# Head statistics of a graph layer, computed through TensorE and PSUM instead of on VectorE

## The chip, the cores and the metric

The kernel runs on one core of one Trainium2 chip. The metric is the device time of one launch in microseconds (us), the median of three runs. The core has five engines with queues of their own: TensorE (PE in the profile, its weight loads PEld), VectorE (DVE), ScalarE (ACT), GpSimd (POOL) and SyncE (SP), which only issues DMAs. They meet through semaphores.

## The reference, cut to what matters

The input x has 3125 rows (nodes) of 256 numbers; 53125 edges (src, dst, sorted by dst) carry three numbers each.

```
xn  = layernorm(x)
gnn = xn + segment_sum(messages(xn[src], edge_attr), dst)      # the edge loop
mix : heads of 32 columns (H = 8, hc = 32), q = xn
      k = (q - mean) / (std(ddof=1) + 1e-5) * kw + kb          # per row and head
      v = (q - mean) / (std(ddof=1) + 1e-5) * vw + vb
      out = q @ (k.T @ v / N) + xn
x = x + gnn + mix
x = x + expert_ffn(layernorm(x))                               # top 2 of 8 experts
```

For k and v each row of xn has to be centred and divided by its standard deviation within each of its 8 heads. This is what the text calls the head statistics. The sums over all rows of the products of these normalised rows (two 128x128 blocks) and their column sums are all that the rest needs.

## The kernel before, in words

**Rows.** The 3125 rows lie as 125 partitions by J = 25 tiles of 256 columns. NB = 5 batches of JB = 5 tiles are loaded; ScalarE normalises batches 0 to 2 (L1017), VectorE batches 3 and 4 (L1330), and SyncE writes them to DRAM as `xn_rows` (L455). VectorE then works out the edges' unit vectors (L1336 to L1342), with one square root on ScalarE between (L1034).

**Head stage (about 38 to 79 us of the trace).** Per batch of five tiles: VectorE sums each head (L1365), forms the deviations `dev` (L1366); ScalarE squares them (L1064); VectorE sums the squares (L1372); ScalarE takes the root (L1070); VectorE adds EPS, takes the reciprocal (L1377, L1378) and multiplies into `hx` in two parts (L1383); TensorE adds hx.T @ [hx, 1] for each tile and half into two banks of `ps3` (L699), two 128-column matmuls a tile. Each fp32 matmul is two records in the trace, a transpose is one. `hx` holds one batch, so L1383 waits until TensorE has used the batch before it. Ahead of this TensorE and ScalarE compose the weights of the edge loop from small 64x64 matrices, in turns: TensorE L664 to L685, ScalarE L1042 to L1059 (`lin_t`, `tp_t`, `ba_t`, ..., `w_sc`).

**Edge loop (about 79.6 to 625 us).** G = 104 groups of 512 edges, software pipelined in `step(i, k)`, which each of TensorE, ScalarE and VectorE has in its own order. GpSimd gathers the source rows, four indirect DMAs of 128 rows a group (L556), into a ring of RING = 10 groups `xg`. It needs all of `xn_rows` written, the group's indices in `idx_st` (written by ScalarE in `stage_idx`, L1030, five groups at a time) and the ring's slot free (`turn_sums`, which TensorE raises once a step). Indices of groups 0 to 9 are staged ahead of the loop, those of groups 10 to 14 in step 4, behind everything that ScalarE does in that step:

```
if k + AHEAD >= RING and (k + AHEAD) % HALF == 0:      # AHEAD = 6, HALF = 5
    stage_idx(i, k + AHEAD)
```

VectorE starts a group with its products (L1431, `prod`), two steps ahead of the step's number; nothing of the loop precedes the end of the head stage in the queues of TensorE, ScalarE and VectorE. ScalarE also clears the six parts of the accumulator `agg` in the first steps (L1148).

**After the loop** come the second layernorm and the gate, and then 56 expert tiles, in the order of TensorE (L961, L975).

Of the kernel before, what the change touches and what calls it, by code (L numbers as in the profile page):

```python
# [52 lines left out]
def gps_layer_kernel(nc, t, out, dbg=None):  # L53
# [42 lines left out]

    COLS = 5
# [14 lines left out]
    with ExitStack() as ctx:  # L112
# [32 lines left out]
        dev = sb(early, "dev", [P, J, D])  # L145
        compose = ExitStack()
        wsm = sb(compose, "wsm", [M, len(names), M])
        lin_t = sb(compose, "lin_t", [M, 128])
        tp_t = sb(compose, "tp_t", [M, 2, 128])
        ba_t = sb(compose, "ba_t", [M, 128])  # L150
        d_t = sb(compose, "d_t", [M, 128])
        c_t = sb(compose, "c_t", [M, 128])
        w_v = sb(compose, "w_v", [M, M])
        rep = sb(compose, "rep", [M, 2, 128])
        compose.close()
        sq = sb(early, "sq", [P, JB * H, HC])
# [12 lines left out]
        hx = sb(early, "hx", [P, JB, 2, 129])  # L169
# [40 lines left out]

        loop = ExitStack()
# [96 lines left out]

        PARTS = ((0, 3), (3, JB))
        head_ready, head_used = ([sem(f"{n}{k}") for k in (0, 1)] for n in ("head_ready", "head_used"))  # L310
        kv_ready, sel_padded = sem("kv_ready"), sem("sel_padded")

        class GroupSems:

            def __init__(s, tag, ring):
                s.ring = ring
                s.gathered = [sem(f"{tag}gathered{i}") for i in range(ring)]
                (s.idx, s.prod, s.dot, s.zt_ps, s.zt_sb, s.f_ps, s.o0, s.hid, s.hid_ps, s.hid_t, s.scores, s.neg_top,
                 s.exp, s.hot, s.norm, s.coef, s.eo, s.sel, s.scattered, s.added, s.turn_heads, s.turn_sums) = (  # L320
                    sem(tag + n) for n in ("idx", "prod", "dot", "zt_ps", "zt_sb", "f_ps", "o0", "hid", "hid_ps", "hid_t",
                                           "scores", "neg_top", "exp", "hot", "norm", "coef", "eo", "sel", "scattered",
                                           "added", "turn_heads", "turn_sums"))

        main, wide = GroupSems("", RING), GroupSems("wide_", 1)
        loc_ready, agg_final = sem("loc_ready"), sem("agg_final")
# [71 lines left out]
        def mix_t_ps(s):  # L398

            return ps2[:, 1, s * 512 + 260:s * 512 + 260 + 2 * P].rearrange("q (h p) -> q h p", h=2)  # L400

# [241 lines left out]
        def _(pe):  # L643
# [17 lines left out]
            pe.wait_ge(w_loaded, 16 * len(names))  # L661
            pe.wait_ge(consts_ready, 10)
            pw = ps1[:, 0, :]
            pe.transpose(pw[0:M, 0:M], W["lin_src_w1"], ident[0:M, 0:M])  # L664
            pe.transpose(pw[0:M, M:128], W["lin_src_w0"], ident[0:M, 0:M]).then_inc(w_mm, 1)
            pe.wait_ge(w_copied, 1)
            for k, (a, b) in enumerate((("tp1_w11", "tp1_w00"), ("tp1_w10", "tp1_w01"))):
                o = 128 + 128 * k
                pe.matmul(pw[0:M, o:o + M], W[a], lin_t[:, 0:M], start=True, stop=True)
                mm = pe.matmul(pw[0:M, o + M:o + 128], W[b], lin_t[:, M:128], start=True, stop=True)  # L670
            mm.then_inc(w_mm, 1)
            pe.wait_ge(w_copied, 2)
            pe.matmul(pw[:, 0:M], tp_t[:, 0, :], W["lin_hidden_w0"], start=True, stop=True)
            pe.matmul(pw[0:M, 128:256], W["lin_hidden_w0"], tp_t[:, 0, :], start=True, stop=True)
            pe.matmul(pw[0:M, 256:384], W["lin_hidden_w1"], tp_t[:, 1, :], start=True, stop=True).then_inc(w_mm, 1)
            pe.wait_ge(w_copied, 3)
            pe.matmul(pw[:, 0:M], ba_t[:, :], W["tp2_w00"], start=True, stop=False)
            pe.matmul(pw[:, 0:M], d_t[:, :], W["tp2_w11"], start=False, stop=True)
            pe.matmul(pw[:, M:128], c_t[:, :], W["tp2_w11"], start=True, stop=True)
            pe.matmul(pw[:, 128:192], ba_t[:, :], W["tp2_w01"], start=True, stop=False)  # L680
            pe.matmul(pw[:, 128:192], c_t[:, :], W["tp2_w10"], start=False, stop=True)
            pe.matmul(pw[0:M, 192:256], d_t[:, 0:M], W["tp2_w10"], start=True, stop=True).then_inc(w_mm, 1)
            pe.wait_ge(w_copied, 4)
            pe.matmul(pw[:, 256:320], rep[:, 0, :], w_v[:, :], start=True, stop=True)
            pe.matmul(pw[:, 320:384], rep[:, 1, :], w_v[:, :], start=True, stop=True).then_inc(w_mm, 1)  # L685

            pe.wait_ge(short_ready, 1)
            pe.wait_ge(base_ready, 2)
            pe.transpose(ps1[0:1, 1, 256:384], short[:, 0:1], ident[:, :]).then_inc(short_col, 1)  # L690
            pe.wait_ge(edge_cols_taken, len(tables))
            pe.wait_ge(banks_cleared, 1)
            for b in range(NB):
                for k, (j0, j1) in enumerate(PARTS):
                    pe.wait_ge(head_ready[k], b + 1)
                    for jj in range(j0, j1):
                        for c in range(2):

# [296 lines left out]
        def _(act):  # L995
# [41 lines left out]
            for k in range(0, RING, HALF):  # L1037
                stage_idx(0, k)
# [855 lines left out]
```

## Time and profile before

| | us |
|---|---|
| median of 3 runs | 1160.52 |
| the three runs | 1160.38, 1160.52, 1164.48 |
| span of the profiled execution | 1163.6 |
| TensorE busy | 1056.7 (91%) |
| VectorE busy | 762.1 (65%) |
| ScalarE busy | 623.8 (54%) |
| GpSimd busy | 634.9 (55%) |

The profile is of one execution, whose span, from its first to its last instruction, is 1163.6 us; no other time is listed for it, and it lies 0.9 us under the highest of the three runs and 3.1 us over the median. Starts in the rows count from the start of the span. A share of busy time is a mean over stages that are bound by different things, so the stages are read apart. The granted TensorE clock is given as a share of 2.4 GHz: 1.00 is 2.4 GHz and 0.50 is 1.2 GHz.

### The profile page before, as it was taken

What the parts mean: (1) busy time and instruction counts of PE and PEld (TensorE: products, weight loads), DVE (VectorE), ACT (ScalarE), POOL (GpSimd) and SP (SyncE); (2) the same over time, 40 slices, a digit from 0 to 9 for tenths busy, and PEclk for the clock granted to TensorE, in tenths of its full rate; (3) what the DMA queues carried; (4) which work ended last, traced back from release to release, by engine and by line L of the source; (5) the groups of instructions that cost most, each with busy time, mean ns of one, the idle gap of its engine ahead of it and who ended that gap; (6) DMA issues with size and microseconds to landing.
All of it is one profiled execution on the core that took longest, in us unless ns stands there. A gap on an engine that the chain in (4) does not pass through costs nothing.

```text
span 1163.6 us, 27165 instructions
## 1 busy us (share of the span) xinstructions
PE 1056.7 (91%) x8001; PEld 1003.1 (86%) x8002; DVE 762.1 (65%) x1942; ACT 623.8 (54%) x1948; POOL 634.9 (55%) x700
## 2 busy tenths in 40 slices
PE   1377999999999999999998977799999999999993
PEld 1267999999999999999997975699999999999992
DVE  6888999999999999999984658333333333333330
ACT  3329555555555555555554760655555555555550
POOL 2474777777777777777731300444444444444431
PEclk9568999999999999999997989899999999999997
DMA  6532333333333333333320334583222222222224
GB/s 160 160 91 68 111 109 112 103 108 103 109 113 105 110 109 109 109 111 105 105 61 5 106 117 181 177 296 65 36 36 34 38 36 36 36 36 36 35 29 124
DMA packets 47378, 108.51 MB, mean 93 GB/s; under 512 B 13814, under 2 KB 24871, under 8 KB 45160
## 3 DMA queue, kind: packets, MB, share of 16 engines
q0 software_dynamic: 30720, 69.24, 24.2%
q1 hardware_dynamic: 16308, 37.47, 9.9%
q10 hardware_dynamic: 308, 1.28, 0.3%
q8 instruction: 21, 0.34, 0.1%
q14 instruction: 21, 0.17, 0.0%
HBM read 90.88 MB, written 20.27 MB: 96 GB/s over the span
## 4 chain that ended last, share of the span: by engine, by line
PE 44%; issue 15%; DVE 12%; POOL 10%; ACT 9%; DVEq 4%; DMA 4%; SPq 0%; POOLq 0%; ACTq 0%
PE ps L961 17%; PE ps L975 16%; POOL xg L556 10%; ACT e L1115 5%; DMA xg<-xn_rows,idx_st 3%; DVEq L1551 2%; PE ps L813 1%; PE ps L864 1%; DVE neg_top L1452 1%; PE ps L860 1%; PE ps L945 1%; ACT agg L1148 1%; PE ps L889 1%; PE ps L699 1%; PE ps L861 1%
## 5 line engine op out<-in xcount | busy, mean ns | idle before, releaser
L556 POOL DMA_INDIRECT xg<-xn_rows,idx_st x416 | 417.5, 1004 | 170.3 <-issue 124.6
L813 PE MATMUL ps<-sel,xg 128*128 128x120 f32 x2496 | 298.5, 276 | 3.8 <-DVE sel L1540 1.3
L813 PEld LDWEIGHTS ps<-sel,xg 128*128 128x128 f32 x2496 | 286.8, 192 | 10.0 <-issue 9.2
L1266 ACT ACTIVATE ht_sb<-ps,b_cur 128x128 f32<-128x128 f32 x448 | 127.9, 369 | 162.5 <-PE ps L961 162.5
L961 PEld LDWEIGHTS ps<-xst,w_st 128*128 128x128 f32 x1792 | 210.1, 193 | 5.6 <-issue 2.8
L961 PE MATMUL ps<-xst,w_st 128*128 128x128 f32 x1792 | 210.6, 276 | 2.3 <-ACT ht_sb L1266 1.7
L1115 ACT ACTIVATE e<-ps,neg_top 128x65 f32<-128x65 f32 x416 | 125.4, 316 | 161.8 <-DVE neg_top L1452 143.7
L975 PE MATMUL ps<-w_sb,ht_sb 128*128 x896 | 202.8, 379 | 0.8 <-DVE y_sb L1845 0.8
L626 POOL DMA_INDIRECT sum_rows<-y_sb,put_st x56 | 108.4, 1935 | 145.6 <-DVE y_sb L1848 135.4
L975 PEld LDWEIGHTS ps<-w_sb,ht_sb 128*128 128x128 f32 x896 | 166.7, 191 | 21.4 <-issue 1.2
L1845 DVE TENSOR_TENSOR y_sb<-ps,b_bc 128x256 f32<-128x256 f32 x56 | 23.8, 425 | 184.2 <-PE ps L975 184.2
L1256 ACT ACTIVATE w_st<-w_sb 128x1024 f32 x56 | 116.1, 2074 | 33.3 <-DVE etile L1813 32.3
L741 PE MATMUL ps<-w_f,zt 128*128 128x128 f32 x832 | 113.1, 280 | 0.0
L1431 DVE TENSOR_TENSOR prod<-xg,edge_r 128x768 f32<-128x768 f32 x104 | 99.3, 955 | 11.5 <-DMA xg<-xn_rows,idx_st 8.1
L741 PEld LDWEIGHTS ps<-w_f,zt 128*128 128x128 f32 x832 | 104.0, 196 | 0.6
L1540 DVE TENSOR_TENSOR sel<-hot,ps 128x800 f32<-128x800 f32 x104 | 102.2, 982 | 0.3
L1439 DVE TENSOR_REDUCE xg<-prod 128x256 f32<-128x768 f32 x104 | 99.0, 952 | 0.2
L1832 DVE TENSOR_SCALAR w_st<-w_sb 128x1024 f32 x56 | 61.6, 1100 | 42.1 <-PE ps L961 39.1
L612 POOL DMA_INDIRECT xs_sb<-expert_in_rows,take_st x56 | 61.0, 1089 | 48.5 <-POOL take_st L608 48.5
L1115 ACT ACTIVATION_READ_ACCUMULATOR e<-ps,neg_top 128x1 f32 x416 | 85.7, 206 | 0.0
L726 PE MATMUL ps<-ident,xg 128*128 128x128 f32 x416 | 66.3, 283 | 11.2 <-DVE xg L1439 8.8
L1087 ACT ACTIVATE zt<-ps 128x512 f32<-128x512 f32 x104 | 63.5, 611 | 12.4 <-PE ps L726 12.4
(271 smaller groups left out, 1363.1 us busy)
## 6 DMA issues: line engine op xcount, KB each, us to landing
w_sb<-in_L_ffn_W SPq DMA_DIRECT2D x16, 1024.0 KB, 6.8
xg<-xn_rows,idx_st POOLq DMA_INDIRECT x416
x_sb<-in_x SPq DMA_DIRECT2D x5, 560.0 KB
xn_rows<-xn_sb SPq DMA_DIRECT2D x5, 560.0 KB
xn_t<-xn_rows SPq DMA_DIRECT2D x25, 112.0 KB
expert_in_rows<-xf_sb SPq DMA_DIRECT2D x12, 224.0 KB
sum_rows<-x_sb SPq DMA_DIRECT2D x12, 224.0 KB
out<-sum_rows SPq DMA_DIRECT2D x3, 560.0 KB
```

What stands on the lines that cost most here:

```text
L556: pool.indirect_dma_start(xg[:, s, tt, M:M + D], None, xn_dram, bass.IndirectOffsetOnAxis(ap=idx_st[:, s, tt:tt + 1], axis=0)).then_inc(ma ...
L626: pool.indirect_dma_start(sum_dram, bass.IndirectOffsetOnAxis(ap=put_st[:, s:s + 1], axis=0), y_sb[:, s, :], None, compute_op=ALU.add).the ...
L741: mm = pe.matmul(f_bank(s)[:, tt * 128:(tt + 1) * 128], zt[:, s, tt * 128:(tt + 1) * 128], w_f[:, :], start=True, stop=True)
L813: mm = pe.matmul(ps3[:, s, col:col + n], xg[:, r, tt, lhs0:lhs0 + 128], sel[:, s, lo:lo + n], start=(tt == 0), stop=(tt == TG - 1))
L961: mm = pe.matmul(h_of(c), w1_st[:, s, kc, c, :], xst[:, s, kc, :], start=(kc == 0), stop=(kc == 1))
L975: mm = pe.matmul(ps1[:, 1, 0:D], ht_sb[:, o % 2, c, :], w2_sb[:, bass.ds(e, 1), c, :].rearrange("p e d -> p (e d)"), start=(c == 0), stop= ...
L1115: ins = act.activation(e0[:, s, tt, :], score_ps(s)[:, tt * (M + 1):(tt + 1) * (M + 1)], ACT.Exp, bias=neg_top[:, s, tt:tt + 1], accum_out ...
L1256: act.activation(w1_st[:, o % 2, 1, :, :], w1_columns(e, 1), ACT.Copy).then_inc(w1_half1, 1)
L1266: ins = act.activation(ht_sb[:, o % 2, c, :], h_of(c), ACT.Gelu, bias=b1_cur[:, o % 2, c:c + 1])
L1431: return dve.tensor_tensor(prod[:, :, :, :], xg[:, s, :, 128:320].rearrange("p t (u m) -> p t u m", m=3), r, ALU.mult)
L1439: dve.tensor_reduce(xg[:, o % RING, :, 0:M], prod[:, :, :, :], AX.X, ALU.add).then_inc(main.dot, 1)
L1540: return dve.tensor_tensor(sel[:, s, 0:TG * 5 * WIN].rearrange("p (t k w) -> p t k w", t=TG, k=5), hot[:, s, :, :].unsqueeze(2).to_broadca ...
```

## The change

The head stage is laid out anew; what it computes stays the same.

- TensorE transposes each half tile of `xn_sb` into PSUM (`turn_pair`, two tiles at a time, 13 pairs); ScalarE copies the transposed pair to SBUF (`copy_turned`); TensorE multiplies it with the 128x128 matrix `centre` = identity minus the mean over each head, so that the deviations come out in PSUM (`centre_pair`). The tiles are taken in the order 15 to 24, then 0 to 14 (`TURNED`).
- ScalarE takes the squares from PSUM into `sq` (four pairs deep) and copies the deviations from PSUM into `hx`, which now holds all 25 tiles.
- VectorE only sums the squares (`mean_squares`, per pair), and per four tiles adds EPS, takes the reciprocal and multiplies `hx` in place (`quotients`). The head sums of `xn` and `dev` (L1365, L1366) are gone, with the tile `dev` and the waits for one batch's `hx`.
- TensorE's head sums come per four tiles (`head_sums`), from the sixth pair on.
- The composing of the weights is put between the pairs: the first part behind the first two turns, then behind pairs 0, 1 and 3 on TensorE, and the copies behind pairs 0, 1 and 3 on ScalarE. ScalarE stages the indices of the first ten groups behind pair 2 (`stage_first`), where it did so ahead of everything.
- VectorE's small preparations (L1348 to L1355) and the making of `centre` go ahead of the wait for the square root of the edge lengths; the flags and `w_f`, `w_hi`, `w_lo` go between the quotients.
- The small composing tiles now lie over the loop's tiles instead of the head stage's. A few semaphores that the main loop did not use are gone.

```diff
+            turn_lin()
+            pe.wait_ge(edge_cols_taken, len(tables))
+            turn_pair(0)
+            turn_pair(1)
+            compose_first()
+            pe.wait_ge(centre_ready, 1)
+            COMPOSED_AFTER = {0: compose_hidden, 1: compose_second, 3: compose_upper, 4: turn_short}
+            for q in range(NQ):
+                centre_pair(q)
+                turn_pair(q + 2)
+                if q in COMPOSED_AFTER:
+                    COMPOSED_AFTER[q]()
+                if q >= 5 and q % 2 == 1:
+                    if q == 5:
+                        pe.wait_ge(banks_cleared, 1)
+                    head_sums((q - 5) // 2)
+            for f in range((NQ - 5) // 2, NF):
+                head_sums(f)
...
-            act.wait_ge(edges_ready, 1)
-            for k in range(0, RING, HALF):
-                stage_idx(0, k)
...
+            def copy_turned(q):
+                act.wait_ge(rows_turned, q + 1)
+                n = len(PAIRS[q])
+                act.activation(xtt[:, q % 2, 0:n, :, :].rearrange("f t h p -> f (t h) p"),
+                               turned_ps(q)[:, 0:n, :, :].rearrange("f t h p -> f (t h) p"), ACT.Copy).then_inc(turned_copied, 1)
+            def squares(q):
+                act.wait_ge(rows_centred, q + 1)
+                if q >= SQUARES:
+                    act.wait_ge(head_var, q - SQUARES + 1)
+                act.activation(sq[:, q % SQUARES, 0:n, :], centred_ps(q)[:, 0:n, :], ACT.Square).then_inc(head_sq, 1)
+            def deviations_out(q):
+                act.activation(hx[:, 2 * q:2 * q + n, :, 0:128].rearrange("p t c f -> p (t c) f"),
+                               centred_ps(q)[:, 0:n, :].rearrange("p t (c f) -> p (t c) f", f=128), ACT.Copy).then_inc(head_dev, 1)
...
+            copy_lin()
+            copy_turned(0)
+            COPIED_AFTER = {0: copy_first, 1: copy_hidden, 2: stage_first, 3: copy_second}
+            for q in range(NQ):
+                copy_turned(q + 1)
+                squares(q)
+                deviations_out(q)
+                if q in COPIED_AFTER:
+                    COPIED_AFTER[q]()
+                if q >= 3 and q % 2 == 1:
+                    head_deviation((q - 3) // 2)
+            for f in range((NQ - 2) // 2, NF):
+                head_deviation(f)
...
+            dve.scalar_tensor_tensor(out=centre[:, :], in0=head_block[:, :], scalar=-float(N) / HC, in1=ident[:, :],
+                                     op0=ALU.mult, op1=ALU.add).then_inc(centre_ready, 1)
...
-            def heads(b):
-                own(dve.tensor_reduce(total, xh, AX.X, ALU.add))
-                dve.scalar_tensor_tensor(out=dev[...], in0=total..., scalar=-1.0 / HC, in1=xh,
-                                         op0=ALU.mult, op1=ALU.add).then_inc(head_dev, 1)
...
+            def mean_squares(q):
+                dve.wait_ge(head_sq, q + 1)
+                dve.tensor_reduce(hstat[:, 1, 2 * q * H:(2 * q + n) * H],
+                                  sq[:, q % SQUARES, 0:n, :].rearrange("p t (h c) -> p (t h) c", c=HC), AX.X, ALU.add).then_inc(head_var, 1)
+            def quotients(f):
+                dve.wait_ge(head_std, f + 1)
+                own(dve.tensor_scalar(hstat[:, 0, hb], hstat[:, 2, hb], EPS, None, ALU.add))
+                own(dve.reciprocal(hstat[:, 1, hb], hstat[:, 0, hb]))
+                dve.wait_ge(head_dev, FOURS[f][-1] + 1)
+                dve.tensor_tensor(rows, rows, hstat[:, 1, hb]..., ALU.mult).then_inc(head_ready, 1)
...
+            for f in range(NF + 1):
+                if f < NF:
+                    for q in FOURS[f]:
+                        mean_squares(q)
+                if f >= 1:
+                    quotients(f - 1)
+                if f == 3:
+                    upper_weights()
+                if f == 4:
+                    flags()
```

## Rows read from the trace of the kernel before

**Rows 1.** The page, its first line.
```profile
span 1163.6 us, 27165 instructions
```

**Rows 2.** The chain that ended last (start us, us, what), its longest pieces.
```profile
68.27 6.85 PE ps L699 x32
...
302.98 2.73 DMA xg<-xn_rows,idx_st
...
595.44 4.33 DMA xg<-xn_rows,idx_st
```

**Rows 3.** Line L556, the gathers: what ended GpSimd's idle time (us, times).
```profile
L556 POOL DMA_INDIRECT xg<-xn_rows,idx_st x416: 942/946/2270, 41.4 to 595.4; - x139
  issue: 124.6, 409
```

**Rows 4.** Timeline of GpSimd (start us, us, engine, line, [idle before]): gathers 1, 12, 40, 41.
```profile
41.38 2.27 POOL L556 DMA_INDIRECT xg<-xn_rows,idx_st  x1 [32.87 <-DMA xn_rows<-xn_sb]
57.70 1.97 POOL L556 DMA_INDIRECT xg<-xn_rows,idx_st  x1 [0.30 <-issue]
97.40 0.95 POOL L556 DMA_INDIRECT xg<-xn_rows,idx_st  x1 [0.30 <-issue]
109.68 1.37 POOL L556 DMA_INDIRECT xg<-xn_rows,idx_st  x1 [11.33 <-ACT idx_st L1030]
```

**Rows 5.** Timeline of VectorE: a product of group 100.
```profile
583.20 0.96 DVE L1431 TENSOR_TENSOR prod<-xg,edge_r 128x768 f32<-128x768 f32 x1 [0.21 <-DMA xg<-xn_rows,idx_st]
```

**Rows 6.** Groups by form, 20 to 82 us: busy us, mean ns | idle before.
```profile
L1366 DVE SCALAR_TENSOR_TENSOR dev<-hstat,xn_sb 125x1280 f32<-125x1280 f32 x5 | 7.5, 1492 | 0.2
L1372 DVE TENSOR_REDUCE hstat<-sq 125x40 f32<-125x1280 f32 x5 | 7.4, 1481 | 2.5 <-ACT sq L1064 2.5
L1365 DVE TENSOR_REDUCE hstat<-xn_sb 125x40 f32<-125x1280 f32 x5 | 7.3, 1469 | 0.0
L1383 DVE TENSOR_TENSOR hx<-dev,hstat 125x768 f32<-125x768 f32 x5 | 4.8, 960 | 1.7 <-PE ps L699 1.6
L1383 DVE TENSOR_TENSOR hx<-dev,hstat 125x512 f32<-125x512 f32 x5 | 3.4, 688 | 0.7 <-PE ps L699 0.7
L1378 DVE RECIPROCAL hstat<-hstat 125x40 f32<-125x40 f32 x5 | 2.0, 404 | 0.2
```

**Rows 7.** Timeline of ScalarE ahead of the head stage.
```profile
25.15 7.48 ACT L1017 ACTIVATE xn_sb<-x_sb,ln_tmp,rstd 125x256 f32<-125x256 f32 x15 [0.68 <-DVE ln_tmp L1326]
32.54 0.53 ACT L1034 ACTIVATE edge_len<-edge_len 128x416 f32<-128x416 f32 x1
38.35 0.33 ACT L1030 ACTIVATE idx_st<-edge_src 128x20 int32<-128x20 int32 x2 [5.28 <-DVE edge_r L1342]
```

**Rows 8.** Timeline of TensorE and VectorE: head sums, the loop's first product.
```profile
61.82 4.67 PE L699 MATMUL ps<-hx 125*128 125x129 f32 x20 [1.72 <-DVE hx L1383]
76.23 2.50 PE L699 MATMUL ps<-hx 125*128 125x129 f32 x20 [0.23 <-DVE hx L1383]
79.64 0.90 DVE L1431 TENSOR_TENSOR prod<-xg,edge_r 128x768 f32<-128x768 f32 x1
```

**Rows 9.** Groups by form of ScalarE, 110 to 600 us: a 512-column copy from PSUM.
```profile
L1087 ACT ACTIVATE zt<-ps 128x512 f32<-128x512 f32 x97 | 59.2, 611 | 0.0
```

**Rows 10.** Stretches: length, busy PE, PEld, DVE, ACT, POOL, then granted clock, DMA, GB/s.
```profile
38.80:48.00 9.20, 6.91 (x31) 5.62 (x31) 6.57 (x8) 3.23 (x13) 5.41 (x5) 0.50 0.42 106
60.00:67.00 7.00, 4.78 (x21) 4.37 (x20) 6.86 (x10) 1.68 (x4) 5.78 (x5) 0.50 0.29 85
75.00:79.00 4.00, 3.50 (x29) 3.12 (x28) 2.98 (x10) 0.00 (x0) 3.09 (x4) 1.00 0.33 98
88.00:95.00 7.00, 3.59 (x30) 3.19 (x30) 6.22 (x12) 7.00 (x10) 5.48 (x6) 0.99 0.33 94
```

**Rows 11.** Timeline of TensorE, 84.3 to 88.3 us: transposes, then matmuls.
```profile
86.83 1.09 PE L726 MATMUL ps<-ident,xg 128*128 128x128 f32 x4 [0.32 <-ACT zt L1087]
87.71 0.85 PE L741 MATMUL ps<-w_f,zt 128*128 128x128 f32 x4
```

More of the change, by code:

```diff
@@ L95, in gps_layer_kernel @@
     MIX = {0: 0, 3: 1, 6: 2}
+    TURNED = list(range(ACT_NB * JB, J)) + list(range(ACT_NB * JB))
+    PAIRS = [range(q, min(q + 2, J)) for q in range(0, J, 2)]
+    NQ = len(PAIRS)
+    FOURS = [range(q, min(q + 2, NQ)) for q in range(0, NQ, 2)]
+    NF = len(FOURS)
+    SQUARES = 4
     COLS = 5
@@ L144, in gps_layer_kernel @@
         xn_sb = sb(early, "xn_sb", [P, J, D])
[L145 to L156, printed above, removed]
+        hx = sb(early, "hx", [P, J, 2, 129])
         kv_tmp = sb(early, "kv_tmp", [128, 2, 2, 128])
@@ L671, in _ @@
[L671 to L690, printed above, removed]
-            pe.wait_ge(edge_cols_taken, len(tables))
[L692 to L697, printed above, removed]
-                            mm = pe.matmul(ps3[:, c, 0:129], hx[:, jj, c, 0:128], hx[:, jj, c, :], start=False, stop=False,
-                                           skip_group_check=True)
-                    mm.then_inc(head_used[k], 1)
+            def turn_lin():
+                pe.wait_ge(w_loaded, 16 * len(names))
+                pe.wait_ge(consts_ready, 10)
+                pe.transpose(pw[0:M, 0:M], W["lin_src_w1"], ident[0:M, 0:M])
+                pe.transpose(pw[0:M, M:128], W["lin_src_w0"], ident[0:M, 0:M]).then_inc(w_mm, 1)
@@ new lines, in compose_upper, with turn_short, turn_pair @@
+            def compose_upper():
+                pe.wait_ge(w_copied, 4)
+                pe.matmul(pw[:, 256:320], rep[:, 0, :], w_v[:, :], start=True, stop=True)
+                pe.matmul(pw[:, 320:384], rep[:, 1, :], w_v[:, :], start=True, stop=True).then_inc(w_mm, 1)
+            def turn_short():
+                pe.wait_ge(short_ready, 1)
+                pe.wait_ge(base_ready, 2)
+                pe.transpose(ps1[0:1, 1, 256:384], short[:, 0:1], ident[:, :]).then_inc(short_col, 1)
+            def turn_pair(q):
+                if q >= NQ:
+                    return
+                tiles = [TURNED[k] for k in PAIRS[q]]
+                if max(tiles) >= ACT_NB * JB:
+                    pe.wait_ge(xn_ready, max(tiles) // JB - ACT_NB + 1)
+                else:
+                    pe.wait_ge(xn_ready_act, max(tiles) // JB + 1)
+                if q >= 2:
+                    pe.wait_ge(turned_copied, q - 1)
+                for t, j in enumerate(tiles):
+                    for h in range(2):
+                        mm = pe.transpose(turned_ps(q)[:, t, h, :], xn_sb[:, j, h * 128:(h + 1) * 128], ident[0:P, 0:P])
+                mm.then_inc(rows_turned, 1)
@@ L1067, in deviation, with copy_lin @@
-            def deviation(b):
-                act.wait_ge(head_var, b + 1)
-                hb = slice(b * JB * H, (b + 1) * JB * H)
-                act.activation(hstat[:, 2, hb], hstat[:, 1, hb], ACT.Sqrt, scale=1.0 / (HC - 1)).then_inc(head_std, 1)
-            act.wait_ge(w_copied, 4)
-            for b in range(NB):
-                squares(b)
-                deviation(b)
+            def copy_lin():
+                act.wait_ge(w_mm, 1)
+                act.activation(lin_t[:, :], pw[0:M, 0:128], ACT.Copy).then_inc(w_copied, 1)
```

223 lines of the change are left out of this document (128 added, 95 removed).

## The prediction, made before the changed kernel was run

> **What bounds the kernel now.** I read the head of the page first: a span of 1163.6 us [rows 1], 3.1 us over the median of the runs; the sum below is made against the span and then carried to the median. The change ends where the edge loop begins, so the questions are when the loop begins and what the loop hands on of an earlier start.
>
> The chain of waits gives the first half of the answer. Around 68 to 79 us it lies on the head sums of TensorE, from about 303 us to the loop's end it comes back again and again to the landing of gathers [rows 2]. The gathers are issued by GpSimd at a pace of their own: 0.95 us each, and 0.30 us of issue between two, 124.6 us of issue over 409 of them [rows 3], so that four take 5.0 us at least. By the mean of 1004 ns on the page a group of four takes 5.2 us. The loop's later products wait for exactly these [rows 5]. So the loop's end is the end of the gather stream, and that stream has one hole: the gathers of groups 0 to 9 end at 98.35 us (97.40 + 0.95), and group 10 starts at 109.68, 11.33 us later, when ScalarE has staged the next indices in step 4 [rows 4]. Step 4 hangs on the loop's start at 79.64 us [rows 8], 30.0 us before it. From this: an earlier loop by X us moves the 41st gather and with it the whole rest by X, as long as the first 40 gathers are done by then. The first 40 took 57.0 us from 41.38 us [rows 4].
>
> The head stage itself is VectorE's and TensorE's. VectorE spends 7.3 + 7.5 + 7.4 us on three passes, 4.8 + 3.4 on the products and 2.0 on reciprocals [rows 6]: 32.4 of the 39 us from its first head sum to the last head sum on TensorE at 78.73 (76.23 + 2.50) [rows 8]. TensorE's granted clock there is 0.50, that is 1.2 GHz, and only at the end 1.00 [rows 10].
>
> **What is removed.** Two of VectorE's three passes go, 14.8 us, and the waits for one batch's hx, 2.3 us [rows 6]. What VectorE still does (7.4 of squares, some 8 of products, 3 of reciprocals and additions) is 18.5 us, and no longer the bound.
>
> **What is added, TensorE.** I count in records, as the profile does: an fp32 matmul is two, a transpose one. Per tile: 2 transposes, 2 centring matmuls (4), 2 head sums (4), so 10. For 25 tiles 250. Composing and the flag's transpose are 32, as 31 stand in the stretch of composing [rows 10]. Eight transposes (the first two pairs) run at about 27 us, when the tiles of VectorE's batch are normalised and everybody else is busy: free. That leaves 274 records from 33 us on. A record costs 0.107 us at 2.4 GHz (the 20 from 76.23 us took 2.50, less the tail of the last) and 0.213 us at 1.2 GHz (the 20 from 61.82 us took 4.67) [rows 8, 10]. So TensorE alone needs 29.3 us at the full clock and 58.4 us at the half clock. This is the term that decides.
>
> **What is added, ScalarE.** Three passes of 500 or 512 columns a pair from PSUM, by the row of such a copy 0.61 us [rows 9], of which about 0.08 overlap with the next, so 0.53: 1.6 us a pair, against 2.14 us of TensorE at the full clock (20 records) and 4.3 at the half. The shapes with squares, and with gaps of one element in `hx`, are not in the trace; below they can hardly be under 0.53, since the copy passes the same columns; above, L1017 takes 0.49 us for 256 columns (7.48 us for 15) [rows 7], which would be 0.98 a pass and 2.9 us a pair. I take 0.53, from the row nearest in source and size.
>
> **The schedule at the start.** ScalarE is free at 33.1 us (32.54 + 0.53) [rows 7], VectorE's preparations fit into its wait for that root. From there TensorE and ScalarE take turns, since composing is threaded between pairs. In us: copy of `lin_t` to 33.3; first composing matmuls, 5 records at half clock, to 34.5; centring of pair 0, 8 records, 36.2, landed 36.5; squares and copy 37.6; `tp_t` 37.9; composing 8 records 39.8; centring of pair 1 41.5, landed 41.7; squares and copy 42.9; `ba_t` and its neighbours 43.5; composing 13 records, now at the full clock, 45.0; centring of pair 2 45.8; squares and copy 47.2; **indices staged 47.5**; pair 3's three passes 49.2; last copies of weights 50.1; last composing 50.8. Here I chose that the clock rises at about 42 us, since TensorE is then nearly without a gap from 38 us on. If it rises by 37 us, the two marks are 45.8 and 49.1.
>
> **The rest of the head stage.** After 50.8 us there remain 17 tiles of centring (68 records), 13 of transposes (26), all head sums (100), one for the flag: 195 records, 20.9 us at the full clock, and ScalarE with 9 x 1.6 + 0.6 lies under it. At the end the last pairs run dry: reduction 0.6, root 0.2, addition and reciprocal 0.5, product 1.2 us of VectorE in front of the last head sums, of which some 2.1 us are not covered. So 50.8 + 20.9 + 2.1 = 73.8 us, against 78.73 before. **X = 4.9 us** (early clock: 72.2 and X = 6.5).
>
> **The gathers.** Before, indices were there at 38.7 us and the gathers began with the landing of `xn_rows` at 41.38. Now the indices are at the 9th place of ScalarE's queue, and GpSimd, behind them, starts at 47.5: 6.1 us later. The first 40 gathers then end near 47.5 + 57.0 = 104.5. Against this, some of them are drawn out by VectorE: the one at 57.70 us took 1.97 instead of 0.95 [rows 4], beside a pass of L1366. Five such passes go; I take 2 us off (bounds 0 and, all of what the 40 took over 1.25 us each, 7): 102.5. Step 4 comes at 109.7 - 4.9 = 104.8. So the 2.3 us between are what is left of the hole, and the late indices cost nothing yet. They cap what an earlier loop can bring at 109.7 - 102.8 = 6.9 us with the late clock, 8.5 with the early one.
>
> The Trainium skill, GPSIMD Engine Reference (its table of the engine), says that GpSimd shares its SBUF interfaces with VectorE and contends with instructions of two SBUF inputs; the row at 57.70 us agrees. Without the rule the 2 us would be 0, and the sum stays.
>
> **Sum.** The 41st gather moves by -4.9 us, the loop's end with it, and nothing behind the loop changes: span 1163.6 - 4.9 = 1158.7, and at the median 1160.5 - 4.9 = **1155.6 us**. A measurement here tells about 0.5% (5.8 us) from no change, so the likeliest outcome lies just inside "no change".
>
> **Rivals.**
>
> 1. *The clock rises early and stays, the hole closes.* X = 6.5 to 8, capped by the gathers: 1152.5 to 1154.5. For it: TensorE has 3.6 us without a gap from 33.5 us. Against it: in the composing stretch before it had 6.9 us of work in 9.2 and stayed at 0.50 [rows 10]. Chance 0.38.
> 2. *ScalarE becomes the bound.* At 0.98 a pass 9.5 pairs cost 28 us after 50.8 or later: 79 to 80 us, no gain, about 1160 to 1162. For it only L1017, which has a bias and a scale per row and reads SBUF. The same time comes out if the clock falls back twice between pairs, 1.7 to 2.5 us each. Chance 0.10.
> 3. *TensorE stays at 1.2 GHz (the slower side).* Then 33.5 + 58.4 and some 4 us of turns: the head stage ends at 96 us instead of 78.7, step 4 moves by +17, and the time is 1177.7. For it: through all of the old head stage, with 4.8 us of work in 7, the clock was 0.50 [rows 10]. Against it: in the new order TensorE at 1.2 GHz is short of time and never idle after 50 us, and the one stretch without gaps before, 6.85 us of head sums from 68.27 us, ended at 2.4 GHz [rows 2, 10]. It decides from the point where the clock is still low after 55 us; each 5 us of delay beyond costs 2.5 us, and 10 us of it already take the gain. Chance 0.12.
>
> A transpose might not count as work: 4 of 20 records of a steady pair. In the trace the clock was back at 0.99 from 88 us [rows 10], right after a stretch with four transposes among matmuls [rows 11], so here they do not keep it down. The Trainium skill, TensorE: Matmul & The Clock Gate (Part 4: PE-mode transpose), says that the full clock does not engage for transposes. By that rule rival 3 would be the outcome; the trace speaks against it, which is why its chance is 0.12 and not more.
>
> **How the numbers follow.** The forecast as worked out, a gain of 2.5 to 5.8 us, has 0.40; rival 1 has 0.38, all of it over 0.5% faster; rival 2 has 0.10, no change; rival 3 0.12, slower. So faster 0.38, no change 0.50, slower 0.12. The range: down to the cap, 1160.5 - 8.5 = 1152; up over rival 2 and the scatter of the runs, 1163. Rival 3 is left outside.
>
> **What would show it.** The granted clock between 33 and 60 us (rises by 37 or 42: right; later: rival 3). ScalarE's 38 passes near 0.6 us each. The first gather at 46 to 48 us. The last head sum ending at 72 to 75.5 us. Most of all the idle time in front of the 41st gather: 1 to 4 us instead of 11.33, with the gather itself at 103 to 106. The forecast is wrong in its second half if that gather moves and the loop's end does not, which would mean that the loop's pace was TensorE's after all.

## The result, and the profile after: 12 us slower

| | before | changed |
|---|---|---|
| median of the runs, us | 1160.9 (1160.4 to 1164.5, 4 runs) | 1172.9 (1170.4 to 1175.4, 4 runs) |
| ratio | | 1.0094, 95% interval 1.0076 to 1.0112 |
| profiled execution, us | span 1163.6 | 1173.9, span 1172.1 |
| first gather starts, us | 41.38 | 50.95 |
| first product of the loop, us | 79.64 | 77.34 |
| 41st gather, us | 109.68 | 107.66 |
| last product of the loop, us | 599.79 | 610.78 |
| from there to the end, us | 563.8 | 561.3 |

Up to the 41st gather the change does what was forecast of it, by less: the first product of the loop comes 2.3 us earlier, the 41st gather 2.0 us. Then the loop takes 533.4 us from its first product to its last instead of 520.2. The page of the changed kernel: its span, the queues, and the group of the loop's first instruction on VectorE (busy us, mean ns | idle before).

```profile
span 1172.1 us, 27534 instructions
...
q14 instruction: 57, 0.47, 0.1%
q8 instruction: 22, 0.36, 0.1%
...
L1547 DVE TENSOR_TENSOR prod<-xg,edge_r 128x768 f32<-128x768 f32 x104 | 99.0, 952 | 28.9 <-issue 27.4
```

The products used to wait for gathers at the end [rows 5]; now the idle time before them ends by "issue": nothing that the profile shows. The view of the tile `prod` says how often, and the timeline of VectorE where (start us, us, ..., [idle before]); the two products shown are the first ones of two turns of the rolled loop, which holds ten groups.

```profile
  issue: 27.4, 7
  DMA xg<-xn_rows,idx_st: 1.2, 2
```
```profile
171.76 0.42 DVE L1721 TENSOR_TENSOR x_sb<-x_sb,mixed 125x256 f32 x1
176.13 0.96 DVE L1547 TENSOR_TENSOR prod<-xg,edge_r 128x768 f32<-128x768 f32 x1 [3.95 <-issue]
...
229.88 0.96 DVE L1547 TENSOR_TENSOR prod<-xg,edge_r 128x768 f32<-128x768 f32 x1 [4.07 <-issue]
```

Seven waits, at groups 20, 30, ... 80: each time VectorE's program jumps back to the start of its loop, at 3.7 to 4.1 us a time. (The trace has 322 instructions of VectorE from one of these jumps to the next, in both kernels.) The chain of waits (start us, us, what) now has these pieces where it had gathers [rows 2]:

```profile
172.17 3.62 issue
225.79 3.76 issue
279.47 3.73 issue
333.15 3.69 issue
```

The page holds the second clue. Queue q14, "instruction", carries 57 packets; in the kernel before it had 21. Between 180 and 530 us, in the midst of the loop, it has 33 of some 8 KB in the changed kernel and one in the kernel before:

```profile
q14 instruction: 33, 0.27, 0.3%
```

Two of the packets start inside the first wait, at 172.9 and 173.3 us, and it is so at all seven. The view of the queues from 172 to 174.2 us:

```profile
q14 instruction: 2, 0.02, 3.4%
```

So VectorE fetches its loop anew in each turn. Of the 27.4 us only 13.3 reach the loop's end. The old loop had slack to give: its products came 5.00 us apart from group 20 to 37 and 5.15 us apart from 37 to 90, where they waited for gathers, and a VectorE that is late for its own reasons doesn't pay this. The profiled spans differ by -2.3 + 13.3 - 2.5 (behind the loop) = +8.5 us. The medians differ by 12, since the profiled span before lies 2.7 us over the median of its runs and that of the changed kernel 0.8 us under. The 2.5 us behind the loop are hardly the change's: e3 below, the old code but for two instructions, took 560.9 us there.

The head stage in the changed kernel. First the timeline of TensorE: three rows of centring, each of four calls (8 records), then the last head sums. Behind it the timeline of GpSimd: the first, 40th and 41st gather.

```profile
40.32 2.07 PE L748 MATMUL ps<-centre,xtt 128*125 128x128 f32 x8
...
46.77 2.07 PE L748 MATMUL ps<-centre,xtt 128*125 128x128 f32 x8
...
49.46 1.04 PE L748 MATMUL ps<-centre,xtt 128*125 128x128 f32 x8
...
71.97 4.56 PE L758 MATMUL ps<-hx 125*128 125x129 f32 x36 [1.12 <-DVE hx L1498]
```
```profile
50.95 1.17 POOL L573 DMA_INDIRECT xg<-xn_rows,idx_st  x1 [42.40 <-ACT idx_st L1108]
...
106.28 0.94 POOL L573 DMA_INDIRECT xg<-xn_rows,idx_st  x1 [0.30 <-issue]
107.66 1.04 POOL L573 DMA_INDIRECT xg<-xn_rows,idx_st  x1 [0.44 <-issue]
```

TensorE runs at half speed until about 49 us (2.07 us for what takes 1.04 afterwards), the head sums end at 76.53, and the hole of 11.33 us [rows 4] is closed to 0.44. It is closed mostly from its far side: the first 40 gathers begin 9.6 us later than before, the 41st comes 2.0 us earlier.

### The profile page after: what moved, and what is told of

Its sections match the earlier page's. It is cut to its first block, busy times and chain, and to the rows that moved or that the text cites. A ratio compares the mean times of both kernels' runs of the same rounds, so it can differ in the third digit from the quotient of the medians.

```text
span 1172.1 us, 27534 instructions
## 1 busy us (share of the span) xinstructions
PE 1060.7 (90%) x8151; PEld 1017.0 (87%) x8152; DVE 746.4 (64%) x1942; ACT 640.2 (55%) x1984; POOL 644.6 (55%) x700
## 4 chain that ended last, share of the span: by engine, by line
PE 47%; issue 17%; DVE 13%; ACT 12%; DVEq 7%; POOL 2%; DMA 1%; SPq 0%; ACTq 0%; POOLq 0%
PE ps L1039 17%; PE ps L1053 16%; ACT e L1237 9%; DVEq L1667 4%; PE ps L891 2%; DVE neg_top L1568 2%; POOL xg L573 2%; PE ps L942 1%; DVE prod L1547 1%; PE ps L938 1%; PE ps L1023 1%; DVE norm L1594 1%; DVE ps L1620 1%; PE ps L748 1%; PE ps L967 1%
## 5 line engine op out<-in xcount | busy, mean ns | idle before, releaser
L573 POOL DMA_INDIRECT xg<-xn_rows,idx_st x416 | 426.5, 1025 | 173.1 <-issue 119.4
L1547 DVE TENSOR_TENSOR prod<-xg,edge_r 128x768 f32<-128x768 f32 x104 | 99.0, 952 | 28.9 <-issue 27.4
L819 PE MATMUL ps<-w_f,zt 128*128 128x128 f32 x832 | 116.3, 285 | 0.0
L819 PEld LDWEIGHTS ps<-w_f,zt 128*128 128x128 f32 x832 | 107.2, 202 | 0.0
L804 PE MATMUL ps<-ident,xg 128*128 128x128 f32 x416 | 65.8, 282 | 33.9 <-DVE xg L1555 33.9
L804 PEld LDWEIGHTS ps<-ident,xg 128*128 128x128 f32 x416 | 49.4, 146 | 36.8 <-issue 26.5
```

Source lines behind the costliest of these rows:

```text
L573: pool.indirect_dma_start(xg[:, s, tt, M:M + D], None, xn_dram, bass.IndirectOffsetOnAxis(ap=idx_st[:, s, tt:tt + 1], axis=0)).then_inc(ma ...
L804: mm = pe.transpose(ps1[:, 0, tt * 128:(tt + 1) * 128], xg[:, s, tt, 0:128], ident[:, :])
L819: mm = pe.matmul(f_bank(s)[:, tt * 128:(tt + 1) * 128], zt[:, s, tt * 128:(tt + 1) * 128], w_f[:, :], start=True, stop=True)
L1547: return dve.tensor_tensor(prod[:, :, :, :], xg[:, s, :, 128:320].rearrange("p t (u m) -> p t u m", m=3), r, ALU.mult)
```

## The experiments

**Theory A.** A jump back costs VectorE 4 us when the loop's body lies over one block more of the instruction stream, a block being what is fetched at once. The built programs say that VectorE's loop begins after 255 instructions in the kernel before and after 257 in the changed one, with the same body of 322. The Trainium skill, Runtime: NRT & Kernel Launch (Instruction fetch mechanics), says that an engine's instruction memory is a FIFO refilled by blocks, 32 KiB for 512 instructions on most engines (64 bytes each, worked out from these two figures), and that a taken branch out of the window it holds waits for a fetch. The waits and packets above agree. It speaks of blocks of 16 KiB; in this trace the packets of q14 are of 8192 bytes, which would be 128 instructions, and those of q8 of 16384. In a turn the packets of q14 that are not part of a wait start 20.3 us apart (185.6 and 205.9 us), in which VectorE gets through some 130 of its 322 instructions. A body of 322 fits three blocks of 128 if it starts at a block's 0th to 62nd instruction. The kernel before would stand on the 62nd; what is put ahead of the built program at load isn't known, so only the distance between two places can be read off, not a place by itself.

**Theory B.** The stall comes from something else that the change moved: tiles, semaphores, the longer programs of TensorE (+324 instructions) or ScalarE (+43).

### e1: two instructions fewer ahead of VectorE's loop

```
-            for c in range(2):
-                ins = dve.tensor_reduce(pick_m[:, c, :], pick[:, c, :, :].rearrange("p u m -> p m u"), AX.X, ALU.add)
-            own(ins)
-            for c in range(2):
-                ins = dve.memset(ps3[:, c, 0:129], 0.0)
-            ins.then_inc(banks_cleared, 1)
+            own(dve.tensor_reduce(pick_m[:, :, :], pick[:, :, :, :].rearrange("p c u m -> p c m u"), AX.X, ALU.add))
+            dve.memset(ps3[:, :, 0:129], 0.0).then_inc(banks_cleared, 1)
```

> The changed kernel; VectorE's two clears of the statistics banks are one instruction and its two sums into pick_m are one, so that its loop stands 255 instructions into its program, as in the kernel before (257 in the changed one; the body is 322 in all). Theory A (place in the instruction stream: two more instructions push the end of the loop's body over into one more block of the stream, and each of the 7 jumps back then waits some 4 us for a fetch): no step of over 6 us between first products of neighbouring groups at groups 20, 30, ... 80, no 8192-byte instruction transfers between 180 and 530 us, first product at 77.3, 41st gather at 107.7, the time 1158.5 to 1159.5 us. Theory B (the stall comes from where the tiles now lie, from TensorE's or ScalarE's longer programs, or from semaphores): the seven steps of 9 us stay, 1172 to 1174 us.

Measured: 1159.8 us (1155.6 to 1166.3), before 1162.0 beside it, ratio 0.9983 (0.9963 to 1.0002). Page, q14, what ended the waits of the products, and the product of group 20:

```profile
span 1159.0 us, 27532 instructions
...
q14 instruction: 22, 0.18, 0.0%
```
```profile
  DMA xg<-xn_rows,idx_st: 9.8, 33
  issue: 1.5, 8
```
```profile
172.74 0.96 DVE L1543 TENSOR_TENSOR prod<-xg,edge_r 128x768 f32<-128x768 f32 x1 [0.24 <-issue]
```

The 27.4 us are gone with two instructions, while the first product (77.34) and the 41st gather (107.53) stay. A holds, B falls. The loop now takes 521.1 us.

### e2, e3, e4: 70 more, 2 more in the kernel before, 6 more

```
+        spare_c = sb(graph, "spare_c", [1, 128])
...
             dve.memset(src_raw[96:G, :], 0).then_inc(raw_padded, 1)
+            for k in range(70):      # e2; 2 in the kernel before for e3; 6 for e4
+                dve.memset(spare_c[0:1, k:k + 1], 0.0)
```

> The changed kernel with 70 one-element memsets more on VectorE at 2 us, where it waits for the edge rows until 11.4 us; its loop stands 327 instructions in. Theory A, with transfers of 8192 bytes and so 128 instructions of 64 bytes in one: the loop's body of 322 fits into three such blocks from a start at a block's 0th to 62nd instruction; the kernel before would stand at the very end of that range, two more leave it, and 70 more land in the next block's range: no stalls, 1158.5 to 1159.5 us. Theory A' (any instruction more ahead of the loop is worse than the kernel before; no blocks): stalls stay, 1172. Theory B: stalls stay, 1172 to 1174.

> The kernel before with 2 one-element memsets more on VectorE at 2 us, in its wait for the edge rows; nothing else is changed, so its head statistics are the old ones and its loop stands 257 instructions in, as in the changed kernel. Theory A: the seven steps of 9 us appear at groups 20 to 80, first product at 79.6 as before, last product about 612 to 613, the time 1172 to 1174 us. Theory B: nothing, 1160 to 1161 us.

> The changed kernel with 6 one-element memsets more on VectorE in the same place; its loop stands 263 instructions in. Theory A: still in the bad range (start at a block's 63rd to 127th instruction), the seven steps stay and their size is the same, 1172 to 1174 us, and the fetches in a turn move by 6 of its 322 instructions (1 us). A theory of a lucky place (each even number or each few instructions otherwise): gone or of another size. Theory B: as it is, 1172 to 1174.

Measured: e2 1159.4 us, ratio 0.9979 (0.9965 to 0.9992), no stall. e3, the old kernel with its old head statistics and two instructions more, 1175.6 us, ratio 1.0118 (1.0094 to 1.0142), 1.6 us over the highest of the forecast. e4 1173.7 us (one run). What ended the products' waits in e3, then in e4:

```profile
  issue: 27.9, 7
  DMA xg<-xn_rows,idx_st: 1.3, 2
```
```profile
  issue: 20.2, 7
  DMA xg<-xn_rows,idx_st: 2.2, 2
```

So the stall needs nothing of the change, and more instructions also mend it. The tile `spare_c` is in all of these, with a stall and without, so it is not the cause. One thing was missed: in e4 the wait is 2.9 us a turn, not 4. The number of fetches stays (33 between 180 and 530 us), but their places differ: of the two packets that start inside each wait in the changed kernel (172.9 and 173.3 us for a wait from 172.2), e4 has one 0.9 us ahead of the wait (174.0) and one inside it (175.6, for a wait from 174.9). No run was made to test whether this is the whole of the difference.

### e8: one more in the kernel before

The edit is e3's with one memset.

> The kernel before with one one-element memset more on VectorE at 2 us; its loop stands 256 instructions in. It tells where the edge is. If the kernel before stands at a block's 62nd instruction: the seven steps of 9 us are there, 1173 us. If it stands at the 61st: none, 1160 to 1161, and two more are the first that stall.

Measured: 1179.8 us (one run), 7 us over the forecast and a little over the highest of e3's four (1179.4), with stalls of 3.9 to 4.1 us at all seven turns (28.0 us) and 56 packets on q14. Its loop takes 536.9 us. So the kernel before stood on the last place that fits.

### e9, e10: 63 and 64 more

The edit is e2's with 63 and 64 memsets.

> The changed kernel with 63 one-element memsets more on VectorE at 2 us; its loop stands 320 instructions in. Theory A, now with its edge measured (255 instructions: none, 256: stalls): with blocks of 128 instructions and a body of 322 the stalls last from 256 to 320, so this is the last one that stalls: seven steps of 7 to 9 us, 1170 to 1174 us. If the blocks are larger (256) or the edge has another reason, this and e10 come out alike.

> The same with 64 memsets; the loop stands 321 instructions in. Theory A: the first that does not stall: no step over 6.1 us at groups 20 to 80, 1156 to 1162 us. One memset makes 11 us. Otherwise as e9.

These two, e11 and e12 ran where the kernel before took 1297.7 us: from about 65 us until the loop began TensorE issued its matmuls mostly 0.7, 1.4, 2.1 or 2.8 us apart, in e10 for instance

```profile
78.03 0.37 PE L739 MATMUL ps<-ident,xn_sb 125*128 125x125 f32 x1 [0.93 <-issue]
79.44 0.80 PE L759 MATMUL ps<-hx 125*128 125x129 f32 x2 [1.04 <-issue]
```

and the first product came at 115 and 121 us. The times, 1336.0 and 1335.6, therefore tell nothing, and the forecast numbers of both were missed. The jump itself can still be read; the product of group 20 in e9, then in e10:

```profile
234.16 0.96 DVE L1550 TENSOR_TENSOR prod<-xg,edge_r 128x768 f32<-128x768 f32 x1 [5.42 <-issue]
```
```profile
235.21 0.96 DVE L1550 TENSOR_TENSOR prod<-xg,edge_r 128x768 f32<-128x768 f32 x1 [0.28 <-issue]
```

At the seven turns e9 waits 5.0 to 5.8 us, e10 0.1 to 0.3; q14 carries 58 packets in e9 and 24 in e10. Stalls at 256, 257, 263 and 320 instructions, none at 255, 321 and 327. From 256 to 320 are 65 places, and with blocks of 128 a body of 322 fits at 63 places (0 to 62) and misses at the other 65.

This confirms that the place in steps of a block decides, but not the block's size, and the expectation of e9 was wrong to say so: with blocks of 256 instructions a body of 322 fits two of them at 191 places (0 to 190) and misses at the other 65, so all of these runs would come out the same. A loop 384 to 448 instructions in, for instance, would tell the two apart (stalls with 128, none with 256), and none was run. For 128 speak the size of the packets and the 20.3 us between them.

### e5, e6, e7: what became of the forecast gain

Without the stall the kernel takes 0.998 of the time before, not the forecast 0.996. These three start from e1. The edit of e6 is eight matmuls whose result nobody reads, to keep TensorE busy in a wait.

```
 # e5, ScalarE's step
-                if k + AHEAD >= RING and (k + AHEAD) % HALF == 0:
+                if isinstance(i, int) and k == 3:
+                    stage_idx(i, RING)
+                elif k + AHEAD >= RING and (k + AHEAD) % HALF == 0 and not (isinstance(i, int) and k == 4):
                     stage_idx(i, k + AHEAD)
 # e6, TensorE, between turn_pair(1) and compose_first()
+            for k in range(8):
+                pe.matmul(ps2[:, 1, 0:128], ident[:, :], ident[:, :], start=True, stop=True)
```

> The kernel of e1 (changed kernel, VectorE's loop back at 255 instructions), and ScalarE stages the indices of groups 10 to 14 one step sooner (after the scores of group 1, at about 101 us instead of 106.3); nothing else. The 41st gather then waits for whichever is last of the gather before it (103.5 us in e1's profile), the staged indices and the release of its buffer at about 103.9. Theory A (the loop's end hangs on the gather stream, and its one hole is 4.0 us in e1): the 41st gather at 103.9 to 104.2 instead of 107.5, and the end 3.3 to 3.6 us sooner than e1's, 1155 to 1157 us. Rival C (with the hole gone, the loop is bound by VectorE at 5.0 us a group from a product at 77.3 us): the end moves by less, but VectorE's own floor (10th product at 122.6, then 93 steps of 4.99) is 586.7 against 598.5 for the last product, so C decides only if it moves by more than 10 us.

> The kernel of e1, and eight 128x128 f32 matmuls on identity into a bank that nobody reads, in TensorE's wait for lin_t (29.6 to 34.1 us). Theory D (the matmuls of the head stage go at half speed until 49.4 us because TensorE stood idle ahead of them; kept busy, it is at full speed some 12 us sooner): the centring matmuls of the second pair (2.07 us in the changed kernel) take 1.04, the first gather starts at 46 to 47 instead of 48.4 to 51, the first product is at 72.5 to 75 instead of 77.3, the 41st gather at 102 to 105, the time 1154.5 to 1157. Rival E (the half speed has a cause that more matmuls do not mend): as e1, 1158.5 to 1160, or 0.3 us later where the eight run over.

> e5 and e6 together. Theory A with D: the first gather at 46 to 47, the 40th ended at 101.5 to 102.5 and the 41st right behind it, the first product at 72.5 to 75, no hole left in the gather stream; the time 5 to 6 us under e1's, 1153 to 1155. With E instead of D: as e5.

Measured: e5 0.9988 (0.9975 to 1.0002), e6 0.9989 (0.9967 to 1.0011), e7 0.9964 (0.9945 to 0.9982). The 41st gather in e1, then in e5 (timeline of GpSimd):

```profile
107.53 1.20 POOL L573 DMA_INDIRECT xg<-xn_rows,idx_st  x1 [4.03 <-PE ps L804]
```
```profile
107.33 0.94 POOL L573 DMA_INDIRECT xg<-xn_rows,idx_st  x1 [1.05 <-PE ps L804]
```

The times of e5 (1161.1 us) and e7 (1158.6) and the median of e6 (1161.2) all missed their forecasts (1155 to 1157, 1153 to 1155, 1154.5 to 1157).

e5 was mis-forecast: I had the buffer free at 103.9 us. The indices did come 5.2 us sooner, 24.1 us behind the first product instead of 29.3 in e1 (ScalarE's timeline, e5, then e1):

```profile
101.44 0.23 ACT L1108 ACTIVATE idx_st<-edge_src 128x20 int32<-128x20 int32 x1
```
```profile
106.32 0.29 ACT L1108 ACTIVATE idx_st<-edge_src 128x20 int32<-128x20 int32 x1
```

The gather still starts 29.7 us behind the first product, against 30.2 in e1: it waits for TensorE's step that frees the buffer (its last part is L804).

e6's profiled execution has a better head stage than forecast, first product 71.37 and 41st gather 101.57. But the loop takes 523.6 us instead of 521.1 in e1, so that this execution took 1158.5 us, and the ten runs scatter from 1153.6 to 1164.8. In e5 and e7 the loop takes 522.1 and 522.3 us. From group 60 to 100 the products of these three come 5.18 to 5.20 us apart, against 5.12 to 5.13 in the kernel before, e1 and e13; why isn't known. e7's profiled execution, the slowest of its ten, shows where some of the scatter comes from: the clock fell again from 33.6 to 50.7 us, and the first product came at 79.44. The eight calls lasted 2.46 us there, about half of the wait that they were to fill, 4.7 us.

### e11 to e14: both waits of TensorE filled

```
+            for k in range(16):      # against e6
+                pe.matmul(ps1[:, 0, 384:512], ident[:, :], ident[:, :], start=True, stop=True)
             turn_lin()
...
-            for k in range(8):      # behind turn_pair(1)
+            for k in range(14):
 # e12 and e14 also: e5's edit, and stage_first() behind the second pair instead of the third
```

> The kernel of e1 and matmuls on identity that nobody reads in both of TensorE's waits: 16 calls from 19.5 us (until it turns lin's weights) and 14 from 28.6 (until lin_t). In e6 the eight calls lasted only half of the wait once the clock had risen, and e6 and e7 came out otherwise by when it rose and fell (full from 32.7 us in e6, half again from 33.6 to 50.7 in e7). Theory D: with both waits filled the clock is full from 33 us on in every run: first gather 45, first product 71 to 72, 41st gather 101 to 102, and the end 1155 to 1157.5, 3 us under e1's median of its runs. Rival E (the early clock does not carry to the end, since the gather stream or the work behind the loop takes it back): first product at 71 to 72 all the same, the time as e1, 1159 to 1161.

> e11, with e5's sooner indices of groups 10 to 14, and the indices of groups 0 to 9 staged behind the second pair instead of the third. First gather at 42.5 to 44 us, the 40th ended at 98 to 100, the 41st right behind it at 98 to 100 (buffers are free from about 98), no hole; from the 41st gather the runs so far need 582.9 to 587 us more: 1152.5 to 1155 with its 1.7 us around the span 2 more at most. It should beat both kernels; with rival E it comes out at e7's 1158.6.

> The kernel of e11 once more, since e9 to e12 ran where TensorE's matmuls came out at 0.7 to 2.8 us from one to the next between 56 and 96 us, and the kernel before took 1297.7 us. Theory D: clock full from 33 us, first gather 45 to 46.5, first product 71 to 72, 41st gather 101 to 102, 1155 to 1157.5 us against 1160 to 1163 of the kernel before. Rival E: first product the same, time as e1 (0.998 of before), the stream of gathers or what lies behind the loop gives it back.

> The kernel of e12 once more. First gather at 41.3 (as in e12), the 40 gathers' 51 to 56 us behind it end at 92 to 97; the 41st waits for its buffer, some 27 us behind the first product: 98 to 99. Time from the 41st gather to the end of the span 582.9 to 587: 1151 to 1156 us with what lies around the span, ratio to before 0.992 to 0.996. Rival F (VectorE and not the gather stream is then the bound of the loop): 10th product at 117, 93 steps of 4.99: last product not under 581 against a gather-bound 589; F would show as no wait ahead of the products, and is not expected to decide. With rival E: 0.996 to 0.998.

Measured: e11 1327.0 and e12 1326.8 us against 1297.7, ratio 1.0215 for both (1.0176 to 1.0255; 1.0186 to 1.0244), under the same restraint of TensorE as e9 and e10. All four kernels run in this state lost to the kernel before, by 2 to 3%; that a head stage with more work on TensorE is the reason is likely but not shown, since the kernel before has no profile in this state and the loop too is longer in it (647.4 us in e11). e13, the same kernel as e11: **1156.3 us** (1155.5 to 1157.2), before 1162.3, ratio 0.9952 (0.9934 to 0.9970). e14: 1157.6 us, 0.9967 (0.9955 to 0.9979). Timeline of e13: three centring groups of TensorE, first product, 41st gather:

```profile
37.67 1.14 PE L748 MATMUL ps<-centre,xtt 128*125 128x128 f32 x8
42.24 2.07 PE L748 MATMUL ps<-centre,xtt 128*125 128x128 f32 x8
44.94 1.05 PE L748 MATMUL ps<-centre,xtt 128*125 128x128 f32 x8
...
72.84 0.89 DVE L1547 TENSOR_TENSOR prod<-xg,edge_r 128x768 f32<-128x768 f32 x1
```
```profile
103.16 1.02 POOL L573 DMA_INDIRECT xg<-xn_rows,idx_st  x1 [0.45 <-issue]
```

and the 41st gather of e14, whose first 40 were done at 97.09 us:

```profile
105.06 0.95 POOL L573 DMA_INDIRECT xg<-xn_rows,idx_st  x1 [7.97 <-PE ps L808]
```

Rival C did not decide: in e13 31 products still waited for gathers, 8.9 us in all.

Theory D holds in its direction and not in full. With filled waits the granted clock is 1.00 from 31.3 us in e13 and from 32.6 in e14, but in both it falls again for 3.4 us (41.5 to 45.0 in e13, hence the 2.07 at 42.24), and in e14 a second time (49.7 to 53.1). The first product comes at 72.8 and 75.3 us; in the five profiled executions of the same head stage without filled waits (the changed kernel, e1, e2, e4, e5) it lies between 75.7 and 79.6. In e13 the gain reaches the end: the last product is 5.3 us earlier than in e1, by a first product 4.5 us earlier.

e14 missed its forecast (41st gather at 98 to 99, 1151 to 1156 us): its gathers are there earlier and wait 8 us for a buffer whose release hangs on the loop's start. e13 beats the kernel before by 0.5%. Against e1 it was not run on the same chip, and the intervals of the two ratios still touch. It is the best version found.

## Why the prediction was wrong, by its own steps

**The step that failed is in the sum: "The 41st gather moves by -4.9 us, the loop's end with it".** The gather moved by -2.0 us, the loop's end by +11.0. The forecast put at nothing what the change does to the loop itself. I counted what each engine executes ahead of the loop, not how many instructions it has there. The count on VectorE went from 255 to 257, which put the loop's body over one block more, and 27.4 us of waits for the program came in, 13.3 of them at the loop's end. e1 takes them out with two instructions, e3 and e8 bring them into the old kernel with two and with one, e9, e10 and e2 show the other end of the range. Neither the forecast nor a rival had it; rival 3, the slower side, had another mechanism (TensorE at 1.2 GHz for good) and did not occur. The sign that the prediction named did occur, the gather moved and the loop's end did not follow, but not for the reason given there (a pace set by TensorE): the waits are VectorE's.

**The 41st gather moves with the loop's start: right.** In the twelve profiled executions outside e9 to e12 the first product lies between 71.4 and 79.6 us and the 41st gather 29.7 to 30.9 us behind it. The reason given was half of it: in e1, e5 and e14 the wait ends by the step of TensorE that frees the buffer, and indices staged 5.2 us sooner moved the gather by half a microsecond (e5).

**The loop's end moves with that gather: right to about 3 us, once the stall is out.** From the 41st gather to the last product: 490.1 us before, 490.9 in e1, 490.0 in e2 and e13, but 491.4 in e14 and 492.4 to 493.4 in e5, e6 and e7. A gain of 2 to 8 us in the head stage can lose up to 3 of them there.

**When the clock rises: mis-sized here, and not the same in each execution.** Forecast 42 us, measured 49.4. The granted clock on the page is no help for this stretch: the trace holds no clock record before 49.4 us, and the view prints 1.00 while the matmuls have 0.21 us a record (columns as in [rows 10]):

```profile
34.00:48.00 14.00, 12.47 (x56) 10.89 (x57) 6.38 (x6) 4.85 (x14) 0.00 (x0) 1.00 0.54 158
```

TensorE was busy for 12.47 of these 14 us, much as I had taken it to be, and the clock did not rise. In e1, with the same head stage, it rose at 42.3 us and fell again at 45.8. One composing call (2 records) in the changed kernel, then the same call in e1 and a row of centring behind it:

```profile
44.04 0.69 PE L706 MATMUL ps<-wsm,ba_t 64*128 64x64 f32 x2 [0.82 <-ACT c_t L1133]
```
```profile
43.44 0.43 PE L706 MATMUL ps<-wsm,ba_t 64*128 64x64 f32 x2 [0.90 <-ACT c_t L1133]
...
46.92 1.92 PE L748 MATMUL ps<-centre,xtt 128*125 128x128 f32 x8
```

In e2 it rose at 42.5 and fell for 3.4 us at 45.9, in e4 it was low until 50.6, and e5 has a row of 1.91 us still at 48.86. So a forecast of one time for the rise could not be right for all executions: over these five the first product lies at 75.7 to 79.6 us and X between 0.0 and 3.9 us. What decides between an early and a late rise was not found. What hangs on it in the profiled execution: indices 49.8 instead of 47.5, end of the head stage 76.5 instead of 73.8, X 2.3 us (the first product; the preparations ahead of the stage were 0.8 us late besides) instead of 4.9. Where the rise came by 33 us (e6) X was 8.3, beyond rival 1.

**ScalarE's passes: right.** 0.57 to 0.63 us each. **TensorE's records at the full clock: right.** 17.1 us without a gap from 52.9 us:

```profile
52.90:70.00 17.10, 17.10 (x156) 17.01 (x156) 13.19 (x27) 12.11 (x28) 13.49 (x12) 1.00 0.32 93
```

**The first 40 gathers: right in length** (56.3 us against 55 in the sum), late in place: 107.22 us at the end instead of 102.5. The 41st stands 0.44 us behind them, so the cap on what an earlier loop can bring, forecast at 6.9 us, was reached at 2.0. It cost next to nothing: in e1, where the gathers were done 4.03 us ahead, the 41st came only 0.13 us earlier. In e13, where indices come sooner with the clock, it was reached at 6.5 (109.68 - 103.16).

**Transposes as work for the clock.** The forecast gave rival 3 a chance of 0.12. In the stretch above, with four transposes in each pair's records, the speed stayed full for 17.1 us. By the rule that the prediction takes from the Trainium skill, TensorE: Matmul & The Clock Gate (Part 4: PE-mode transpose), the full clock does not engage for transposes; among matmuls, as here, it did not decide. In e1, e4, e7 and e14 the clock did fall once more for 3.4 us between 49 and 58 us, and no run tells what part the transposes had in that.

## What to carry to other kernels

A loop in an engine's program has a place in its instruction stream, and an edit ahead of it, of one instruction, can cost more than the work it saves. Before comparing two versions count the instructions ahead of each engine's loop and in its body, and look at the instruction queues and at "issue" waits that come once a turn; keep the loop's start in the middle of the range that fits, not on its edge. When a change makes TensorE the driver of a short stage, what it does in the waits ahead of that stage bears on the speed of the stage, and this speed can differ from one execution to the next: look at more than one profile.
